# A fused two-layer decoder on one core: turned value product in the second cross attention, and one key tile in float

## The reference, cut to what matters

```python
scores = jnp.einsum('bhqd,bhkd->bhqk', qh, kh) / math.sqrt(hd)      # hd = 32, Sq = 512, Sk = 1024
causal = jnp.arange(Sk)[None, :] <= jnp.arange(Sq)[:, None] + (Sk - Sq)
scores = jnp.where(causal[None, None], scores, -10000.0)
attn = jax.nn.softmax(scores, axis=-1)
out = jnp.einsum('bhqk,bhkd->bhqd', attn, vh)
x = _layernorm(x + out)
```

## Time and profile before

| | |
|---|---|
| time, median of 3 runs | 2269.06 us (2265.43 to 2271.65) |
| the profiled execution | 2268.35 us, span 2266.3 us |
| PE busy | 1987.9 us (88%) |
| DVE busy | 1448.3 us (64%) |
| ACT busy | 1079.4 us (48%) |
| POOL busy | 602.4 us (27%) |
| mean granted clock of TensorE | 0.944 of 2.4 GHz |

### The profile page before, as it was taken

The page is one execution under the profiler, slowest core; times in us unless marked ns, Lnnn a source line. Parts: engine busy times, 40 slices in busy tenths (PEclk is TensorE's granted clock), DMA queues, the critical chain, the costliest instruction groups (busy, mean ns, idle before and its releaser), DMA issues. The chain is left out here.

```text
span 2266.3 us, 32930 instructions
## 1 busy us (share of the span) xinstructions
PE 1987.9 (88%) x11168; PEld 1193.0 (53%) x11168; DVE 1448.3 (64%) x2728; ACT 1079.4 (48%) x2150; POOL 602.4 (27%) x510
## 2 busy tenths in 40 slices
PE   7888878969999799977999999996698886799998
PEld 4555544447777477753545445452355543355553
DVE  5666666376775577765848566577699965555334
ACT  4666634232334233332726355471898893345332
POOL 3555500032331333300101001011645450123220
PEclk8999988988999799998999999997799997999999
DMA  4000003020110211004110010004600003466533
GB/s 137 25 25 1 1 18 136 1 72 28 43 46 1 71 47 46 23 0 137 38 38 21 22 52 0 1 1 87 158 1 2 1 1 114 156 175 191 137 71 89
DMA packets 95792, 125.26 MB, mean 55 GB/s; under 512 B 8926, under 2 KB 52254, under 8 KB 95662
## 3 DMA queue, kind: packets, MB, share of 16 engines
q1 hardware_dynamic: 88942, 107.79, 15.7%
q0 software_dynamic: 6720, 15.73, 3.8%
HBM read 101.68 MB, written 18.61 MB: 53 GB/s over the span
## 5 line engine op out<-in xcount | busy, mean ns | idle before, releaser
L1170 POOL TENSOR_TENSOR wl<-stage,wh 128x512 fp32r<-128x512 f32 x80 | 117.3, 1498 | 395.2 <-DVE wh L1161 395.2
L1429 POOL TENSOR_TENSOR Zl<-z,Zh 128x512 f16<-128x512 f32 x32 | 51.1, 1598 | 493.8 <-ACT Zh L1590 493.8
L77 PE MATMUL PS<-XTh,wh 128*128 128x512 f16 x416 | 160.0, 385 | 19.8 <-ACT t L2013 19.0
L1270 ACT ACTIVATE h<-PS,bup 128x512 f32<-128x512 f32 x64 | 44.2, 690 | 277.9 <-PE PS L79 277.9
L78 PE MATMUL PS<-XTl,wh 128*128 128x512 f16 x416 | 159.6, 384 | 0.0
L79 PE MATMUL PS<-XTh,wl 128*128 128x512 f16 x416 | 159.4, 383 | 0.0
L2476 POOL TENSOR_TENSOR PTl<-P,PTh 128x512 f16<-128x512 f32 (+2 forms) x128 | 116.4, 920 | 124.3 <-ACT PTh L2648 124.2
L2647 ACT ACTIVATE P<-PS 128x512 f32<-128x512 f32 (+3 forms) x256 | 135.1, 528 | 21.6 <-PE PS L2573 19.8
L2648 ACT ACTIVATE PTh<-PS 128x512 f16<-128x512 f32 (+3 forms) x256 | 136.2, 532 | 0.0
L2663 DVE TENSOR_REDUCE M<-PS 128x1 f32<-128x640 f32 (+3 forms) x128 | 127.1, 1012 | 4.5 <-PE PS L2549 4.5
L2476 DVE TENSOR_TENSOR PTl<-P,PTh 128x512 f16<-128x512 f32 (+1 forms) x128 | 96.1, 756 | 50.0 <-ACT PTh L2648 48.7
(11 more groups left out here) (378 smaller groups left out, 5872.0 us busy)
## 6 DMA issues: line engine op xcount, KB each, us to landing
stage<-in_ffn_W SPq DMA_DIRECT2D x18, 1024.0 KB, 5.4
stage<-in_ffn_Wg SPq DMA_DIRECT2D x9, 1024.0 KB, 5.5
stage<-in_ffn_Wup SPq DMA_DIRECT2D x16, 512.0 KB, 3.9
stage<-in_ffn_Wdn SPq DMA_DIRECT2D x16, 512.0 KB, 3.6
wq<-in_attn_wq SPq DMA_DIRECT2D x4, 1024.0 KB, 5.9
C<-in_ctx SPq DMA_DIRECT2D x8, 512.0 KB, 8.9
stage<-in_ffn_Wsw SPq DMA_DIRECT2D x16, 256.0 KB, 3.5
stage<-in_attn_WV SPq DMA_DIRECT2D x16, 256.0 KB, 4.1
```

Source lines behind the costliest of these rows:

```text
L77: pe.matmul(out, a[0], b[0], start=start, stop=False, skip_group_check=True)
L1170: nc.gpsimd.tensor_tensor(piece(wl[q], ch), piece(st, ch), plain(piece(wh[q], ch)), ALU.subtract).then_inc(w_lo, 1)
```

## The change

The value product is turned round. The exponentials become the stationary operand (128 keys x 128 queries) and V the moving one: for each pair of key tile and query tile `PTh` times the high V with its column of ones (33 columns), `PTh` times the low V (32), `PTl` times the high V (33). Z then lies with queries on the partitions, 4 x 33 columns, in bank 6 or 7 by the parity of the head. The copy `Zs`, the constant `comb` and the combination go.

Key tile 3 (`WHOLE`) of each head is no longer split. ACT makes one float exponential of it into `PF` (two buffers), V's tile 3 is kept as float in `VF`, and PE multiplies them with four float matmuls. The split tiles are seven per head; `SLOTS` goes from 4 to 5 and `RING` from 12 to 10.

The maxima are stored so that one transpose turns all 16 rows of a group (16 x 128), and the shift rows are made in that shape. The heads of a group lie side by side in `QS` and `KS`. DVE's output of head n - 2 moves from kt = 4 to kt = 2 of loop n, and all square roots of the norm come after ACT's loop.

```diff
-    SLOTS = 4
-    RING = CT + 4
+    SLOTS = 5
+    RING = CT + 2
+    WHOLE = 3
+    SPLIT = [kt for kt in range(CT) if kt != WHOLE]
+    ZW = DV + 1
...
+        PF = sb("PF", [P, 2, S], F32)
+        VF = sb("VF", [P, B, H, ZW], F32)
...
+        def z_bank(n):
+            return c.PS[:, 6 + n % 2, 0:QT * ZW].rearrange("p (q e) -> p q e", q=QT)
+        def turned_bank(n):
+            return c.PS[0:GS * QT, 6 + n % 2, QT * ZW:QT * ZW + P]
...
-                        sp.dma_start(QS[b][to, h4::4, :], qp[rows, :, b * S:(b + 1) * S]).then_inc(stack_in[b * 4 + h4], 16)
+                        sp.dma_start(QS[b][to, h4 * GS:(h4 + 1) * GS, :], qp[rows, :, b * S:(b + 1) * S]).then_inc(stack_in[b * 4 + h4], 16)
...
+            nc.gpsimd.memset(VF[:, :, :, DV:ZW], XS).then_inc(ones_done, 1)
...
-            for t in range(B * CT):
-                pool.wait_ge(v_hi, 2 * t + 2)
+            for i, t in enumerate(t for t in range(B * CT) if t % CT != WHOLE):
+                pool.wait_ge(v_hi, 2 * i + 2)
...
-            def turn_maxima(g):
+            def turn_maxima(g, n):
                 pe.wait_ge(max_done, QT * GS * (g + 1))
-                need(pe, z_out, GS * (g + 1) - LEAD - 1)
-                for qt in range(QT):
-                    last = pe.transpose(c.PS[0:GS, 7, qt * P:(qt + 1) * P], M[:, b, qt, h:h + GS], c.ident[:])
-                last.then_inc(m_turned, 1)
+                need(pe, z_out, n - 1)
+                pe.transpose(turned_bank(n), M[:, g].rearrange("p j q -> p (j q)"), c.ident[:]).then_inc(m_turned, 1)
...
             def value_tile(n, kt):
+                if kt == WHOLE:
+                    pe.wait_ge(exp_done, CT * n + kt + 1)
+                    for qt in range(QT):
+                        last = pe.matmul(z_bank(n)[:, qt, :], PF[:, n % 2, qt * P:(qt + 1) * P], VF[:, b, h, :], start=False,
+                                         stop=False, skip_group_check=True)
+                    last.then_inc(z_done, 1)
+                    return
                 wait_lo(pe, n, kt)
                 if kt == 0:
-                    need(pe, z_copied, n)
-                pe.matmul(c.PS[0:VW, 6, cols], v, PTh[:, slot, cols], start=(kt == 0), stop=False, ...)
-                last = pe.matmul(c.PS[0:VW, 6, cols], v, PTl[:, slot, cols], start=False, stop=(kt == CT - 1), ...)
+                    need(pe, z_out, n - 1)
+                    pe.wait_ge(m_shift, 1 + sum(turn_group(i) is not None for i in range(n + 1)))
+                for qt in range(max(kt - K0, 0), QT):
+                    q = slice(qt * P, (qt + 1) * P)
+                    pe.matmul(z_bank(n)[:, qt, :], PTh[:, slot, q], v[:, DV:VW], start=(kt == 0 and qt == 0), ...)
+                    pe.matmul(z_bank(n)[:, qt, 0:DV], PTh[:, slot, q], v[:, 0:DV], start=False, ...)
+                    last = pe.matmul(z_bank(n)[:, qt, :], PTl[:, slot, q], v[:, DV:VW], start=False, ...)
                 last.then_inc(z_done, 1)
-            def combine(n):
...
-                    nc.scalar.activation(Zs[:, n % 2, :], c.PS[0:VW, 6, :], ACT.Copy).then_inc(z_copied, 1)
...
+                    if kt == WHOLE:
+                        need(act, z_done, CT * (n - 2) + kt + 1)
+                        nc.scalar.activation(PF[:, n % 2, :], c.PS[:, 4 + i % 2, :], ACT.Exp, scale=SC).then_inc(exp_done, 1)
+                        continue
...
-                    if n < N and kt not in ON_POOL:
+                    if n < N and kt in SPLIT and kt not in ON_POOL:
                         low_part(dve, nc.vector, n, kt, lo_dve)
...
-                    if kt == 4 and n >= 2:
+                    if kt == 2 and n >= 2:
                         output(n - 2)
```

More of the change, by code:

```diff
@@ L2499, in _ @@
             for t in range(B * CT):
-                need(sp, v_lo, t - SLOTS + 1)
+                before = t - SLOTS
+                if before >= 0 and before % CT == WHOLE:
+                    sp.wait_ge(vf_done, before // CT + 1)
+                elif before >= 0:
+                    sp.wait_ge(v_lo, split_index(*divmod(before, CT)) + 1)
                 sp.dma_start(P32[:, t % SLOTS, :], c.inp["ctx"][t // CT, (t % CT) * P:(t % CT + 1) * P, :]).then_inc(ctx_in[t % SLOTS], 16)
@@ L2538, in max_tile @@
             def max_tile(n, qt):
-                b, h, _ = head(n)
+                b, _, h = head(n)
                 i = QT * n + qt
@@ L2582, in value_tile @@
-                cols = slice(first_query(kt), S)
-                v, slot = V[:, b * CT + kt, h, :], (CT * n + kt) % RING
-                pe.matmul(c.PS[0:VW, 6, cols], v, PTh[:, slot, cols], start=(kt == 0), stop=False,
-                          skip_group_check=True)
-                last = pe.matmul(c.PS[0:VW, 6, cols], v, PTl[:, slot, cols], start=False, stop=(kt == CT - 1),
-                                 skip_group_check=True)
-                last.then_inc(z_done, 1)
-            def combine(n):
-                pe.wait_ge(z_copied, n + 1)
-                need(pe, z_out, n)
-                pe.wait_ge(m_shift, 1 + sum(turn_group(i) is not None for i in range(n + 2)))
-                for qt in range(QT):
-                    last = pe.matmul(c.PS[:, 7, qt * (DV + 1):(qt + 1) * (DV + 1)], Zs[:, n % 2, qt * P:(qt + 1) * P],
-                                     comb[:], start=True, stop=True, skip_group_check=True)
-                last.then_inc(c_done, 1)
+                    need(pe, z_out, n - 1)
@@ new lines, in value_tile @@
+                    pe.wait_ge(m_shift, 1 + sum(turn_group(i) is not None for i in range(n + 1)))
+                v, slot = V[:, b * CT + kt, h, :], split_index(n, kt) % RING
+                for qt in range(max(kt - K0, 0), QT):
+                    q = slice(qt * P, (qt + 1) * P)
+                    pe.matmul(z_bank(n)[:, qt, :], PTh[:, slot, q], v[:, DV:VW], start=(kt == 0 and qt == 0), stop=False,
+                              skip_group_check=True)
+                    pe.matmul(z_bank(n)[:, qt, 0:DV], PTh[:, slot, q], v[:, 0:DV], start=False, stop=False,
+                              skip_group_check=True)
+                    last = pe.matmul(z_bank(n)[:, qt, :], PTl[:, slot, q], v[:, DV:VW], start=False,
+                                     stop=(kt == qt + K0), skip_group_check=True)
@@ L2604, in _ @@
                 if n == GS:
-                    turn_maxima(0)
-            pe.wait_ge(ones_done, 2)
-            pe.wait_ge(v_lo, B * CT)
-            for n in range(N + 2):
+                    turn_maxima(0, 0)
+            pe.wait_ge(ones_done, 3)
+            pe.wait_ge(v_lo, B * len(SPLIT))
+            pe.wait_ge(vf_done, B)
+            for n in range(N + 1):
                 for kt in range(CT):
@@ L2658, in max_tile @@
             def max_tile(n, qt):
-                b, _, h = head(n)
                 i = QT * n + qt
```

111 lines of the change are left out of this document (55 added, 56 removed).

## The result

The changed kernel takes 2252.03 us (median of 4 runs, 2251.1 to 2255.05) against 2268.86 for the kernel before on the same chip: ratio 0.9929, interval 0.9912 to 0.9946. It is faster by 17 us, where the forecast said 37, and the time lies 1 us above the range. The gain is clear of the noise, but under 1%. The profiled execution took 2252.38 us, span 2250.6, mean granted clock 0.931 (before 0.944).

The account below looks back on a forecast made before the run. No engine alone was the bound, but a ring of waits between PE and ACT, 7.96 us a head. Loop 31.6, start 3.7 and tail 2.0 sum to 37.3 us off 2268.35, so 2231, range 2220 to 2251.

Parts of the forecast that it names:

- rival B: Second cross attention's loop: the clock falls to 1.2 GHz and doubles PE's work, +84, 2352 us; chance 3%.
- rival D: The float block takes 1.53 us, the extra 0.72 all on the ring: 22 us over 31 heads, 2253 us; chance 10%.
- float block: Four float matmuls for value tile 3 on PE, ahead of score tile 4: 0.81 us, bounds 0.20 to 1.53.
- the ring: Chain of waits between PE and ACT in each head, taken to set its period: 7.96 us before, 7.02 after.
- Moments: Four moments of the norm on DVE, 1 us each, meet less slack in the loop: -1 us of gain.
- Shift rows: DVE's three steps every fourth head, about 0.2 us each: of 1.07 us extra some 0.25 stays, gain 4.8.
- sum of 31.6: Forecast gain of the loop, us: heads with maxima 22.6, shift rows 4.8, last six heads 5.2, moments -1.
- start: Ahead of the loop, POOL makes low parts of fourteen V tiles instead of sixteen, with five slots: gain 3.7 us.
- end: Tail behind the loop: roots ready earlier, last head's output follows four normalisations; 2.0 us gained at the row of 1877.81.
- A: 66 new stationary loads a head on PE, about 0.1 us each, are not hidden: +72, 2340 us; chance 2%.
- E: The change doesn't do what it says: another wait holds the head at 7.9 us; chance 2%.
- C: DVE becomes the bound in the loop: low parts grow 0.2 each, 7.3 us a head, 2238 us; chance 15%.

Follow-up runs that it names:

- e1: Changed kernel with added products of 252 columns, whose result nobody reads, placed where PE waits; 2244.97 us, ratio 0.9901 to the kernel before.
- e2: As e1, but each added product of 252 columns replaced by four of 33 columns; 2243.18 us, ratio 0.9875 to the kernel before.
- e16: Changed kernel with the norm's moments moved to loops 26 to 29 and half as many added products as e12; 2236.49 us, ratio 0.9848.
- e5: e3 with added products of 252 columns where PE waits, eight more in each loop with moments; 2238.36 us, ratio 0.9856.
- e9: e5 with the norm's moments moved to loops 26 to 29, without the eight additions belonging to them; 2232.05 us, ratio 0.9845.
- e12: Changed kernel with added products much as in e1 and the norm's moments moved to loops 26 to 29; 2238.26 us, ratio 0.9869.
- e11: Changed kernel with the norm's moments moved from loops 20 to 23 to loops 26 to 29, nothing added; 2249.37 us, ratio 0.9911.
- e17: e16 with the turn of the maxima behind value tile 4 on PE and DVE's three steps in loop step 4; 2236.11 us, ratio 0.9846.
- e3: Changed kernel without the float tile: all eight key tiles split again, 12 slots in the ring buffer; 2240.95 us, ratio 0.9864.
- e18: e9 with the turn of the maxima and DVE's three steps in step 4, and slightly fewer additions; 2230.62 us, ratio 0.9831.
- e15: e12 with the turn of the maxima behind value tile 3 instead of 5, DVE's steps two earlier; 2240.02 us, ratio 0.9862.

## Why the prediction was wrong

*The failed step is the clock in the loop.* The forecast put it at 1.00 throughout and gave 3% to rival B, in which it falls; measured were 0.91 in the middle of the loop and 0.53 at its end. The forecast read the clock of the earlier trace rows as a property of the stage, and took the one row with a fall, behind a wait of 1.99 us, as its condition; "the longest I expect in the loop is 0.5". Both halves failed. The longest waits were 1.25 (PE on a row maximum beside the moments) and 1.09 (PE on `mt`), and in the last six heads the clock fell without any long wait: its waits there, from 1814 to 1828, are none above 0.4:

```profile
PE PS L2592 <- ACT PTh L2675: 2.8, 9, 0.4
```

What I had in hand and did not use: by the forecast's own figures PE had 6.88 us of work in 7.96 before and 5.71 in 7.02 after, and in the last six heads the turned product takes the same 1.2 us net of 5.3 from it. Taking work from PE where others set the pace is what uncovered the clock. Additions that only give PE work brought it back, whether wide or narrow (e1, e2) and at half the amount (e16). That is shown. What decides when it falls is not. Neither the share of waits nor the longest one does by itself: the kernel before held 1.00 in its last heads, 1832 to 1869, with 5.6 us of waits in 37 (15%), while the changed one lost it with 12.4 in 120 (10%); and waits of 1.09 us stand in e5, e9, e12 and e16 without a fall.

Rival B's price was wrong too: it reckoned with half clock everywhere, +84. It comes in stretches; the loop lost at least 8.5 us (e11 to e12), and 10.9 by e16 (235.4 to 224.5). That is about half of the 19.6 us that the loop fell short. The time lies only 1 us above the range, and next to rival D's 2253, by chance: the float block was 0.87, not D's 1.53.

*Terms that were mis-sized.* Moments: -1 in all; moving them took 4.4 us off their four heads in e9 against e5 (with eight products a head less), and 3.9 in e12 against e1 (one fall of the clock less). Shift rows: 0.25 each by the forecast, 0.79 measured, and 0.25 once PE no longer waits for `mt` (e17, 7.34 against 7.09). That the 0.25 comes back is partly luck: one of DVE's three steps, put at 0.2 us, takes 1.18 in e17. What the forecast missed is who waits for the first step; it looked only at DVE's slack. The first head took 9.97 instead of about 6.9, at half clock until about 1632; at full clock it takes 7.02 (e11). The forecast's sum of 31.6 also leaves out the 0.3 us that it gave to this head.

*Right by the rows.* Heads of 7.09 (7.02), turned step 0.025, no wait for Z, float block 0.87 (0.81) on the ring ahead of score tile 4, ACT waiting for it; last heads 6.5 to 6.65 before the fall (6.4); start 3.6 by the first tile 7 (3.7); end 2.4 at the forecast's row (2.0). Rivals A and E are out, D too (0.87, not 1.53), and C for the changed kernel, since DVE waits in each plain head:

```profile
1659.68 0.85 DVE L2495 TENSOR_TENSOR PTl<-P,PTh 128x384 f16<-128x384 f32 x1 [0.90 <-ACT PTh L2675]
```


*The conclusion that the forecast could have drawn.* It never priced the float tile by itself. By its own figures a kernel without it would have been held by DVE's 7.13 us, so the tile was worth 0.11 us a head (7.02). e3 measures 6.93 without it and 7.09 with it: the float tile costs 0.16 us a head, and the rest of the change gives more than the whole (22 us of loop against 12).

## What to carry to other kernels

When PE is not the bound and a change takes work from it, ask whether the clock will hold, and leave it work in its waits: here 4 to 8 idle products a head were worth 8 to 11 us of the loop. For each small step added to an engine with slack, look who waits for it; slack of the engine says nothing on that. Time both halves of a two-part change by themselves before both are kept.

## What the runs showed of the hardware

The granted clock was 0.50 or 1.00 and fell in kernels whose PE was 88% busy in the records (177 of 200 us), hardly less than the 90% of before at 1.00: the busy figure of narrow matmuls, 0.18 us shown for steps of 0.025, hides how often PE stands (by its steps PE works about 5.8 us in a head of 7.09, 81%). After the wait that ended at 1727.26 the half clock shows from about 1728 on; the head with it took 10.07 us instead of 7.88.

That falls came at some shift rows and not at others, in one execution, is shown by the heads; what decides between them is open. The Trainium skill, "TensorE: Matmul & The Clock Gate", HAM oscillation, tells of a clock that falls behind idle gaps of PE longer than any in this loop. The runs go beyond that: the longest waits in these loops were 1.09 us on `mt` and 1.0 to 1.3 us beside the moments, in the last six heads 0.4, and the clock fell all the same.

A cast of 16x128 on DVE took 0.22 us in the changed kernel and 1.19 in e17 (medians of 8), at another place of the loop. The traces show what goes with it. In the six heads of e17 with shift rows the cast starts 0.04 us behind the start of a POOL low part of 1.16 us and ends 0.07 us behind its end (1666.57 to 1667.75 on DVE, 1666.52 to 1667.68 on POOL). In the six of e18 it starts 0.3 us ahead of the end of a POOL low part, again ends 0.07 behind it, and takes 0.40. In the six of e15, where POOL does nothing at that time, it takes 0.2. So the traces have the cast waiting for POOL's instruction to end; no run that moves POOL's work alone was made.
